# Linear attention with the values stationary in two column halves, denominators from running key sums, and new orders of all engines

## The chip, the cores and the metric

One NeuronCore of one Trainium2 chip runs the whole program. The metric is the device time of one execution in microseconds (us); lower is better. Matmuls run on PE (TensorE, weight loads shown as PEld), the other engines are DVE (VectorE), ACT (ScalarE), POOL (GpSimd) and SP (SyncE, which here only issues DMAs).

## The reference, cut to what matters

A small audio tower over 64 sequences of 256 frames (252 after a five-tap convolution), width 128: softmax attention with 8 heads and a top-2 mixture of 8 experts (layer 0), then a causal linear attention, a causal two-head attention and a dense mixture of 8 experts (layer 1). Only the linear attention is changed. In the notation of the reference:

```
q = elu(x @ W_q.T) + 1            # 8 heads of 16
k = elu(x @ W_k.T) + 1            # 8 heads of 16
v = x @ W_v.T                     # 8 heads of 64
num[t] = sum over s <= t of (q[t] . k[s]) * v[s]
den[t] = max(q[t] . (sum over s <= t of k[s]), 1e-6)
out = (num / den) @ W_out.T
```

## The kernel before, in words

Two sequences form a pair; a pair is 504 tokens in four tiles of 126 (TOK, TILES, TILE). There are 32 pairs. Everything before a pair's layers (the convolution and its normalisation) is done in a first phase; then three stretches follow: a start, 30 equal rounds, an end. A round works on four pairs at once: the softmax queries and keys of pair r+2 (letter q), the softmax attention of pair r+1 (a), the linear and the causal attention of pair r (l), and the experts' hidden chunks (h) and output chunks (o) of pairs r-1 and r+1.

Each engine has its own written-out order of these parts: a string of letters (SP_ROUND, POOL_ROUND, ACT_ROUND, DVE_ROUND, PE_ROUND and the same for START and END). Each letter runs the next step of that part's generator, up to its next `yield`; every engine works its steps strictly in that order, and counting semaphores join the engines. So a step that waits holds everything behind it on its engine. The letter w in PE_START is a filler matmul (L1713).

Steps that the prediction speaks of, by line:

- h on PE is three f16 matmuls of 504 columns into `pf` (L1315 to L1317, the helper `mm3`, which multiplies f32 numbers kept as a high and a low f16 half); ACT applies the GELU (L897), DVE casts the high half (L1285), POOL subtracts for the low half (L701).
- o on PE is four mm3 of 128 columns, 12 records, into bank 2 of `pf`. There is one such bank, so after an expert's last chunk the next expert's first chunk waits for DVE to add the bank to the residual (L1299, semaphore `gated`). An expert has four chunks in layer 1 and two in layer 0.
- Linear attention on PE, before: scores of four head blocks at a time (L1549, f16, 12 steps a pair, bank 0 of `pa1`). DVE multiplies the diagonal blocks by the causal mask (L1194), ACT copies the others (L845). Then eight steps of six f32 matmuls each (L1568) take the 126x126 factors as the stationary operand and 65 columns as the moving one: 64 value columns of one head and a column of ones, whose product is the denominator. DVE takes the denominator's maximum, its reciprocal and the product for every one of the eight (L1175, L1178, L1184) and writes `o1` with tokens on partitions.
- Output projection, before: four times, PE transposes 128 columns of `o1` (four f32 transposes, L1361), ACT writes the high half (L755), DVE the low half (L987), and PE multiplies by the output weights (L1315 to L1317 on `ot_hi`, `ot_lo`).
- POOL sets the column of ones each round (L685). The values come out of PSUM by ACT (L837).
- The causal attention's value product (L1645, `causal_values`) already has the form that the change brings to the linear one: for each key tile, the values of head 0 and of head 1, 64 columns each, are stationary in one half of the array's columns each, and write PSUM partitions 0 to 63 and 64 to 127.
- SP stores the high and low halves of queries and keys to DRAM and loads them spread over partitions (L494, L498, L504, L510). The softmax scores of the next round (L1422) wait for those of pair r+2. SP also issues the store of the output (L490).

## Time and profile before

| | us |
|---|---|
| median of 3 runs | 4110.01 (4109.32 to 4114.44) |
| the profiled execution, device time | 4117.0 |
| its span, first to last instruction | 4115.3 |
| mean granted PE clock | 0.994 |
| PE busy | 3969.7 (96%) |
| DVE busy | 3329.8 (81%) |
| ACT busy | 2840.7 (69%) |
| POOL busy | 2549.7 (62%) |

Busy time of PE counts a matmul from its start to its modelled end, and matmuls overlap in the pipeline. What a matmul costs is therefore the distance from its start to the next one's start, not its own duration.

### The profile page before, as it was taken

To read this page: it belongs to the slowest core of one execution; us is meant where nothing else is said; L and a number is where in the kernel's file an instruction comes from. 1 tells how busy PE (TensorE), PEld (TensorE's weight loads), DVE (VectorE), ACT (ScalarE), POOL (GpSimd) and SP (SyncE) were. 2 spreads that over 40 slices of the span, in tenths; PEclk is the share of its full clock that TensorE was granted. 3 is DMA by queue.
4 is the path that set the end of the run, shared out by engine and by line. 5 is a ranking of instruction groups with operands and counts; after the bars stand their busy time and mean duration, and the time that the engine had idled before them with its cause. 6 is when DMAs were issued, how large, how long until landed. Compare 5 with 4: busy or idle time off the path is not lost.

```text
span 4115.3 us, 104222 instructions
## 1 busy us (share of the span) xinstructions
PE 3969.7 (96%) x40901; PEld 2888.2 (70%) x40901; DVE 3329.8 (81%) x9263; ACT 2840.7 (69%) x4857; POOL 2549.7 (62%) x2496
## 2 busy tenths in 40 slices
PE   9889999999999999999999999999999999999988
PEld 4457677777767777777777777777777777777766
DVE  4478888888888888888888888888888888888866
ACT  4347777777777777777777677777767777777744
POOL 2246666666666666666666666666666666666646
PEclk9999999999999999999999999999999999999989
DMA  6111110001111010111101011110001111001100
GB/s 183 46 29 29 32 32 27 22 17 32 32 32 32 20 28 17 32 32 32 32 17 30 18 32 32 32 32 17 22 27 32 32 32 31 17 19 29 30 16 6
DMA packets 137273, 127.63 MB, mean 31 GB/s; under 512 B 29008, under 2 KB 135568, under 8 KB 136784
## 3 DMA queue, kind: packets, MB, share of 16 engines
q1 hardware_dynamic: 136784, 120.97, 10.2%
q8 instruction: 324, 5.31, 0.5%
q14 instruction: 165, 1.35, 0.1%
HBM read 71.12 MB, written 49.55 MB: 29 GB/s over the span
## 4 chain that ended last, share of the span: by engine, by line
PE 70%; DVE 20%; DMA 3%; SPq 2%; issue 2%; ACT 2%; POOL 1%; DVEq 0%; ACTq 0%
PE pf L1315 12%; PE pf L1317 11%; PE pf L1316 11%; PE pa L1568 9%; DVE h L1299 4%; PE pa L1460 3%; PE pa L1361 3%; DVE hid_hi L1285 3%; PE pa L1315 3%; PE pa L1317 3%; PE pa L1316 3%; PE pa L1549 3%; PE pa L1446 3%; DVE row_max L1247 2%; SPq L510 2%
## 5 line engine op out<-in xcount | busy, mean ns | idle before, releaser
L701 POOL TENSOR_TENSOR hid_lo<-hid,hid_hi 128x504 f16<-128x504 f32 x1536 | 1789.2, 1179 | 889.5 <-DVE hid_hi L1285 888.6
L897 ACT ACTIVATE hid<-pf,vec 128x504 f32<-128x504 f32 x1536 | 1025.2, 678 | 505.8 <-PE pf L1317 454.1
L1315 PE MATMUL pf<-w_hi,hid_hi 128*126 128x128 f16 x6144 | 1147.2, 225 | 42.4 <-DVE h L1299 38.3
L1317 PE MATMUL pf<-w_hi,hid_lo 128*126 128x128 f16 x6144 | 1121.9, 221 | 0.0
L1316 PE MATMUL pf<-w_lo,hid_hi 128*126 128x128 f16 x6144 | 1121.5, 221 | 0.0
L1315 PEld LDWEIGHTS pf<-w_hi,hid_hi 128*126 128x126 f16 x6144 | 843.5, 137 | 197.8 <-DVE h L1299 106.1
L1285 DVE CAST hid_hi<-hid 128x504 f16<-128x504 f32 x1536 | 799.1, 540 | 87.4 <-ACT hid L897 87.0
L1316 PEld LDWEIGHTS pf<-w_lo,hid_hi 128*126 128x126 f16 x6144 | 845.4, 138 | 30.3
L1317 PEld LDWEIGHTS pf<-w_hi,hid_lo 128*126 128x126 f16 x6144 | 847.4, 138 | 0.0
L1299 DVE SCALAR_TENSOR_TENSOR h<-pf,gates,h 126x128 f32<-126x128 f32 x2048 | 572.8, 342 | 52.7 <-PE pf L1317 52.5
L665 POOL TENSOR_TENSOR pt<-pt,band 126x262 f32<-126x262 f32 x512 | 358.6, 716 | 373.0 <-ACT pt L803 372.9
L1315 PE MATMUL pf<-xf_hi,w_hi 128*128 128x504 f16 x1536 | 579.2, 377 | 2.3 <-DVE xf_lo L1269 1.1
L1317 PE MATMUL pf<-xf_hi,w_lo 128*128 128x504 f16 x1536 | 577.9, 376 | 0.0
L1316 PE MATMUL pf<-xf_lo,w_hi 128*128 128x504 f16 x1536 | 577.8, 376 | 0.0
L1568 PE MATMUL pa<-v,pt 126*126 126x65 f32 x3072 | 391.4, 278 | 1.5 <-DVE o L1184 1.4
L1568 PEld LDWEIGHTS pa<-v,pt 126*126 126x126 f32 x3072 | 365.0, 193 | 18.4 <-issue 18.3
L803 ACT ACTIVATE pt<-pa 126x504 f32<-126x504 f32 x512 | 278.4, 589 | 139.0 <-PE pa L1446 138.0
L1092 DVE TENSOR_REDUCE minus_max<-pa 126x2 f16<-126x504 f32 x512 | 329.6, 682 | 19.1 <-PE pa L1422 15.9
L897 ACT ACT_TABLE_LOAD x247 | 316.9, 1283 | 4.4
L1317 PEld LDWEIGHTS pf<-xf_hi,w_lo 128*128 128x128 f16 x1536 | 150.0, 98 | 177.5 <-issue 1.3
L1175 DVE TENSOR_SCALAR den<-pa 126x4 f32<-126x4 f32 x256 | 40.9, 160 | 252.9 <-PE pa L1568 251.2
L1194 DVE TENSOR_TENSOR pt<-pa,causal 126x504 f32<-126x504 f32 x256 | 173.3, 677 | 64.2 <-PE pa L1549 62.7
(215 smaller groups left out, 7431.0 us busy)
## 6 DMA issues: line engine op xcount, KB each, us to landing
qk_spread<-terms SPq DMA_DIRECT2D x224, 126.0 KB, 2.6
qk_spread<-terms SPq DMA_DIRECT2D x192, 63.0 KB, 2.3
y_scratch<-hid SPq DMA_DIRECT2D x32, 252.0 KB, 2.1
y_in<-y_scratch SPq DMA_DIRECT2D x32, 252.0 KB, 3.2
terms<-qk_hi SPq DMA_DIRECT2D x32, 252.0 KB, 2.3
terms<-qk_lo SPq DMA_DIRECT2D x32, 252.0 KB, 2.4
qk_spread<-terms SPq DMA_DIRECT2D x32, 252.0 KB
terms<-ot_hi SPq DMA_DIRECT2D x32, 252.0 KB, 2.4
```

The costliest lines, as they stand in the source:

```text
L665: nc.gpsimd.tensor_tensor(strip, strip, band[0:TILE], ALU.mult).then_inc(S0["p_band"], 1)
L701: nc.gpsimd.tensor_tensor(hid_lo[:, c % 8], hid[:, c % HIDS], hid_hi[:, c % 8], ALU.subtract).then_inc(hid_lo_done[c % 2], 1)
L803: nc.scalar.activation(pt[0][0:TILE, i % 8], pa0[0:TILE, i % 2, 0:TOK], ACT.Exp, scale=HEAD ** -0.5).then_inc(S0["p_exp"], 1)
L897: nc.scalar.activation(hid[:, c % HIDS], pf[:, c % 2, 0:TOK], func, bias=vec[:, bias:bias + 1]).then_inc(F["hid_ready"], 1)
L1092: nc.vector.tensor_reduce(minus_max[0:TILE, 2 * b:2 * b + 2, hd // 2, 64 * (hd % 2) + MAX_ROW], pa0[0:TILE, i % 3, 0:TOK].rearrange("p (t ...
L1194: nc.vector.tensor_tensor(pt[1][0:TILE, i % 4].rearrange("p (t q) -> p t q", t=4), pa1[0:TILE, 0, 0:TOK].rearrange("p (t q) -> p t q", t=4 ...
L1285: nc.vector.tensor_copy(hid_hi[:, c % 8], hid[:, c % HIDS]).then_inc(F["hid_hi_done"], 1)
L1299: last = nc.vector.scalar_tensor_tensor(h[0:TILE, i], pf[0:TILE, 2, i * D:(i + 1) * D], gates[0:TILE, kind, i, e:e + 1], h[0:TILE, i], ALU ...
L1315: nc.tensor.matmul(out, ah, bh, start=start, stop=False, skip_group_check=skip)
L1316: nc.tensor.matmul(out, ah, bl, start=False, stop=False, skip_group_check=skip)
L1317: return nc.tensor.matmul(out, al, bh, start=False, stop=stop, skip_group_check=skip)
L1568: last = nc.tensor.matmul(pa1[0:TILE, 1, first:first + wide], factors[:, cols(blk)], v1[0:TILE, 2 * b + kt, hd], start=(t == 0), stop=(t = ...
```

## The change

The scores, the masks and the products with the weights stay. What is new:

- The value product is turned: the values (64 columns of one head, f32) are stationary, two heads in the two column halves, and the factors (126 columns) move. The output has value columns on partitions and tokens along the bank, so it needs no transposes before the output projection. Four steps a pair instead of eight, each of 12 f32 matmuls.
- The denominators come ahead of the attention: PE transposes the keys, ACT and DVE split them in f16 halves, PE multiplies them by a 0/1 matrix `later` (running sums), DVE multiplies by the queries, PE sums over each head's 16 rows by a 0/1 matrix `head_of`, DVE takes maximum and reciprocal once, POOL widens each to 64 columns, PE transposes them (16 f32 transposes) and ACT copies them to `spread_inv`. DVE then divides a whole bank at once, ACT writes the high halves and POOL the low halves.
- The value projections stand between these steps, in banks (1, 1, 1, 0).
- The gate's step semaphores are merged into one (same instructions, same order). New constants are built on POOL at the start.
- All order strings are rewritten (the letters of a round are the same in number but for l: PE 54 to 53, ACT 35 to 40, DVE 47 to 42, POOL 6 to 13).

```diff
-SP_ROUND = ("llallqqoqq")
+SP_ROUND = ("llalloqqqq")
-POOL_ROUND = ("llhhhhlhhhahhhhaaaaaahaaahhhahaaaaaahhhhhahlhhhhhhhlhlhhhqhhhhhhhhhhhhhhh")
+POOL_ROUND = ("llhhhhhhhhllllhhahhaaaaaaaaaalaahhllhaalahahhlhhhhahhlhhlhhhhhhhhhhqhhhhhhhhhhhh")
-ACT_ROUND = ("hhhlhlhllhhlhlhhhlhhllhhalaaaaaaalaahaaalhhaaaahallahhllhhahhhlalhhhllhllahhhahhqhlhqhhqhlllllql"
-             "hlqlhlhhllhhlhh")
+ACT_ROUND = ("hhhlhlhllhhhlhllhllhllhlllhhaalaaaalaalaalaalhhalaalaahhhhahlalhhhlhllalahhahhhahhlhhhhllllqhlhh"
+             "lhqlhhlqlhhlqqlhhhlh")
-DVE_ROUND = ("lalhahaaohlhaahllllallhaahoaaahaahaahhaaaalolhlhhlllhlllhllllhahllolhlalahqlahalaholllhhhhoalhhh"
-             "ahoalahoalhhoqqhhhlollqohlllholhhoqhhlhqlolhqlhohhlho")
+DVE_ROUND = ("llhhahaaoalhaahllllllalhhlohlaahaaaaahaahaalaalhhllolhllllllhalohhhlllhhqahoalahaahhhoahalaaholh"
+             "hahlohhllohhlhollholqqhhhohhqlhhohlqolqlohhqhohl")
-PE_ROUND = ("hhaoohoaohhlaohllhaolohhlaohlhaolaoaohhaaaolahlhalllooallaaalllhallhaallloollhhallaaaloaloahlalh"
-            "lahllloohlhohohooahlohaohllhlloohhoohoohahaoohqlhlohohloqhohloqohlqlollolhlohloqlhoholhhloo")
+PE_ROUND = ("hhohaoohaohlaohllhaooohlhlhllalhllaolalhalloalahlaahloolalalhhlaalalalaaloollloolhaalaallhllhhao"
+            "haoooalhoahhlhllloooahhahohoohohahaooohllohloohhloohoqohloohlhhllohlhqloqhlqoolhoohqlhohol")
```

On POOL:

```diff
-                counted = n(p)
-                pool.wait_ge(started, 1)
-                pool.wait_ge(S1["h_biased"], counted)
-                nc.gpsimd.memset(v1[0:TILE, :, :, LIN_VALUE:LIN_VALUE + 1], 1.0).then_inc(S1["v1_ones"], 1)
-                yield
+                for i in range(TILES):
+                    if i == 0:
+                        pool.wait_ge(S1["inv_ready"], n(p + 1))
+                    nc.gpsimd.tensor_copy(wide[i].rearrange("p (h d) -> p h d", h=HEADS),
+                                          inv_den[0:TILE, i].unsqueeze(2).to_broadcast([TILE, HEADS, LIN_VALUE])
+                                          ).then_inc(S1["inv_wide"], 1)
+                    yield
+                for quad in range(4):
+                    b, g = quad // 2, quad % 2
+                    pool.wait_ge(S1["o1_hi"], n(p * 4 + quad + 1))
+                    part = (slice(None), slice(2 * g, 2 * g + 2), slice(b * SEQ, (b + 1) * SEQ))
+                    nc.gpsimd.tensor_tensor(ot_lo[1][part], fs1[:, quad % 2, 0:TOK].rearrange("p (c q) -> p c q", c=2),
+                                            ot_hi[1][part], ALU.subtract).then_inc(S1["o1_lo"], 1)
+                    yield
```

On ACT (`values_high` runs four times, as `high` did):

```diff
+            def values_high(p, quad):
...
+                act.wait_ge(S1["o1_norm"], n(p * 4 + quad + 1))
+                nc.scalar.copy(ot_hi[1][:, 2 * g:2 * g + 2, b * SEQ:(b + 1) * SEQ],
+                               fs1[:, quad % 2, 0:TOK].rearrange("p (c q) -> p c q", c=2)
+                               ).then_inc(S1["o1_hi"], 1)
...
+                act.wait_ge(S1["keys_turned"], n(p + 1))
+                nc.scalar.copy(keys_hi, pa1[0:TILE, 0, 0:TILES * D]).then_inc(S1["keys_high"], 1)
+                yield
...
+                for k in range(4):
+                    act.wait_ge(S1["spread_raw"], n(p * 4 + k + 1))
+                    nc.scalar.copy(spread_inv[:, k], pa1[:, 1 - k % 2, 0:TOK]).then_inc(S1["spread_ready"], 1)
                     yield
...
-                for c in range(4):
-                    high(1, p * 7 + 1 + c, ot_hi[1][:, c % 2])
-                    yield
```

On DVE (the old `divide` ran eight times, the new one runs four times):

```diff
+                dve.wait_ge(S1["keys_high"], n(p + 1))
+                nc.vector.tensor_tensor(keys_lo, pa1[0:TILE, 0, 0:TILES * D], keys_hi,
+                                        ALU.subtract).then_inc(S1["keys_low"], 1)
+                yield
+                dve.wait_ge(S1["sums_raw"], n(p + 1))
+                nc.vector.tensor_tensor(q_sums, pa1[:, 0, 0:TOK], fs1[:, 0, 0:TOK], ALU.mult
+                                        ).then_inc(S1["sums_ready"], 1)
+                yield
+                dve.wait_ge(S1["den_raw"], n(p + 1))
+                nc.vector.tensor_scalar(den[0:TILE], pa1[0:TILE, 0, 0:TILES * HEADS], 1e-6, None, ALU.max
+                                        ).then_inc(S1["den_done"], 1)
+                dve.wait_ge(S1["den_done"], n(p + 1))
+                nc.vector.reciprocal(inv_den[0:TILE].rearrange("p t h -> p (t h)"), den[0:TILE]
+                                     ).then_inc(S1["inv_ready"], 1)
+                yield
+
+                def divide(quad):
+
+
+                    dve.wait_ge(S1["av_done"], n(p * 4 + quad + 1))
+                    dve.wait_ge(S1["o1_lo"], n(p * 4 + quad - 1))
+                    nc.vector.tensor_tensor(fs1[:, quad % 2, 0:TOK], pa1[:, 1, 0:TOK], spread_inv[:, quad], ALU.mult
                                             ).then_inc(S1["o1_norm"], 1)
...
-                for c in range(4):
-                    low(1, p * 7 + 1 + c, ot_lo[1][:, c % 2], ot_hi[1][:, c % 2])
-                    yield
```

On PE (the four steps of the value projection stand before, between and after these; that of the sums runs for both sequences):

```diff
+                pe.wait_ge(S1["el_map"], n(p * 2 + 2))
+                for i in range(TILES):
+                    last = nc.tensor.transpose(pa1[0:TILE, 0, i * D:(i + 1) * D], fs1[:, 1, cols(i)], ident[:])
+                last.then_inc(S1["keys_turned"], 1)
...
+                pe.wait_ge(S1["keys_low"], n(p + 1))
+                for b in range(2):
+                    for kt, first, width in ((0, 0, SEQ), (1, TILE, TILE)):
+                        for keys in (keys_hi, keys_lo):
+                            last = nc.tensor.matmul(pa1[:, 0, b * SEQ + first:(b + 1) * SEQ],
+                                                    keys[:, (2 * b + kt) * D:(2 * b + kt + 1) * D],
+                                                    later[0:TILE, 0:width], start=(kt == 0 and keys is keys_hi),
+                                                    stop=(kt == 1 and keys is keys_lo), skip_group_check=True)
...
+                pe.wait_ge(S1["sums_ready"], n(p + 1))
+                for i in range(TILES):
+                    last = nc.tensor.matmul(pa1[0:TILE, 0, i * HEADS:(i + 1) * HEADS], q_sums[:, cols(i)], head_of[:],
+                                            start=True, stop=True)
...
+                for k in range(4):
...
+                    for c in range(2):
+                        for t in range(2):
+                            first = c * SEQ + t * TILE
+                            last = nc.tensor.transpose(pa1[:, 1 - k % 2, first:first + TILE],
+                                                       wide[2 * b + t][:, (2 * g + c) * D:(2 * g + c + 1) * D],
+                                                       ident[0:TILE, 0:TILE])
...
+                        pe.wait_ge(S1["at_ready"], n(p * 8 + 2 * quad + 2))
+                        pe.wait_ge(S1["o1_norm"], n(p * 4 + quad))
+                        off = pt[1][0:TILE, 3 * quad % 4]
+                        for c in range(2):
+                            diagonal = pt[1][0:TILE, (3 * quad + 1 + c) % 4]
+                            for t, (kt, qt) in enumerate(((0, 0), (0, 1), (1, 1))):
+                                for odd in range(2):
+                                    factors, blk = (off, 2 * c + odd) if t == 1 else (diagonal, 2 * odd + kt)
+                                    first = c * SEQ + qt * TILE
+                                    last = nc.tensor.matmul(pa1[64 * odd:64 * odd + 64, 1, first:first + TILE],
+                                                            v1[0:TILE, 2 * b + kt, 4 * g + 2 * c + odd],
+                                                            factors[:, cols(blk)], start=(t < 2), stop=(t != 1),
+                                                            skip_group_check=True)
...
-                        turn(1, p * 7 + 1 + c, o1_rows[:, :, c * 128:(c + 1) * 128])
...
+                for c in range(4):
+                    pe.wait_ge(S1["o1_lo"], n(p * 4 + 3 + c // 2))
```

## Rows read from the trace of the kernel before

**Rows 1.** The page: busy us (share of the span) xinstructions of each engine.
```profile
PE 3969.7 (96%) x40901; PEld 2888.2 (70%) x40901; DVE 3329.8 (81%) x9263; ACT 2840.7 (69%) x4857; POOL 2549.7 (62%) x2496
```
**Rows 2.** Timeline, transposes that open a pair's work, one round apart (start, duration).
```profile
1994.52 0.60 PE L1392 MATMUL pa<-ident,pt 128*126 128x128 f32 x4
...
2114.97 0.60 PE L1392 MATMUL pa<-ident,pt 128*126 128x128 f32 x4
```
**Rows 3.** Timeline of PE: the old value product between two score steps.
```profile
2052.75 1.48 PE L1568 MATMUL pa<-v,pt 126*126 126x65 f32 x12
2054.07 0.39 PE L1549 MATMUL pa<-qk_spread 128*126 128x126 f16 x4
```
**Rows 4.** Timeline of PE: four f32 transposes and what follows them.
```profile
2081.86 0.59 PE L1361 MATMUL pa<-ident,o 126*128 126x126 f32 x4
2082.29 0.64 PE L1361 MATMUL pa<-ident,xn 126*128 126x126 f32 x4
```
**Rows 5.** Timeline of PE: the causal value product, in two column halves.
```profile
2010.35 0.86 PE L1645 MATMUL pa<-fs,v 126*64 126x252 f32 x8
2011.14 0.27 PE L1315 MATMUL pf<-w_hi,hid_hi 128*126 128x128 f16 x1
```
**Rows 6.** Timeline of PE: 504-column f16 records, then a half-height form.
```profile
2002.78 0.38 PE L1316 MATMUL pf<-xf_lo,w_hi 128*128 128x504 f16 x1
2002.99 0.38 PE L1317 MATMUL pf<-xf_hi,w_lo 128*128 128x504 f16 x1
2003.30 0.49 PE L1618 MATMUL pa<-pt 64*126 64x126 f32 x4
```
**Rows 7.** Groups by line and form (count | busy us, mean ns | idle before).
```profile
L1175 DVE TENSOR_SCALAR den<-pa 126x4 f32<-126x4 f32 x256 | 40.9, 160 | 252.9 <-PE pa L1568 251.2
L1178 DVE RECIPROCAL inv_den<-den 126x4 f32<-126x4 f32 x256 | 45.6, 178 | 8.8
L1184 DVE TENSOR_TENSOR o<-pa,inv_den 126x256 f32<-126x256 f32 x256 | 108.6, 424 | 8.8
L1299 DVE SCALAR_TENSOR_TENSOR h<-pf,gates,h 126x128 f32<-126x128 f32 x2048 | 572.8, 342 | 52.7 <-PE pf L1317 52.5
L987 DVE TENSOR_TENSOR ot_lo<-pa,ot_hi 128x504 f16<-128x504 f32 x192 | 128.2, 681 | 55.4 <-ACT ot_hi L755 50.6
L755 ACT ACTIVATE ot_hi<-pa 128x504 f16<-128x504 f32 x192 | 109.8, 588 | 132.1 <-PE pa L1361 119.4 <-PE pa L1645 12.5
L897 ACT ACT_TABLE_LOAD x247 | 316.9, 1283 | 4.4
L677 POOL COPY h<-h 126x512 f32<-126x512 f32 x32 | 19.5, 608 | 3.0 <-DVE h L1299 3.0
L701 POOL TENSOR_TENSOR hid_lo<-hid,hid_hi 128x504 f16<-128x504 f32 x1536 | 1789.2, 1179 | 889.5 <-DVE hid_hi L1285 888.6
```
**Rows 8.** Who waited for whom: us in total, times, longest.
```profile
PEld pf L1315 <- DVE h L1299: 106.1, 228, 1.8
PEld pa L1376 <- DVE gate_terms L1027: 45.9, 61, 1.7
```
**Rows 9.** Timeline: softmax keys of one pair, from projection to the scores.
```profile
2007.77 0.38 PE L1315 MATMUL pa<-w_hi 128*128 128x504 f16 x1
...
2015.72 0.73 DVE L1075 SCALAR_TENSOR_TENSOR qk_lo<-pa,vec,qk_hi 128x504 f16<-128x504 f32 x1
...
2016.48 0.36 SPq L498 DMA_DIRECT2D terms<-qk_lo  x1
...
2017.46 1.12 SPq L490 DMA_DIRECT2D out<-h  x2
2018.63 3.22 SPq L504 DMA_DIRECT2D qk_spread<-terms  x5
...
2025.66 0.43 PE L1422 MATMUL pa<-qk_spread 64*126 64x252 f16 x4
```
**Rows 10.** A stretch near the end: us, busy (x) of PE, PEld, DVE, ACT, POOL, clock, DMA, GB/s.
```profile
3980.00:3990.00 10.00, 9.17 (x58) 8.41 (x59) 4.14 (x11) 1.17 (x3) 1.14 (x1) 0.59 0.00 0
```

More of the change, by code:

```diff
@@ L878, in linear_and_causal_attention @@
                     yield
-                high(1, p * 7 + 6, ot_hi[1][:, 0])
+                high(1, p * 3 + 2, ot_hi[1][:, 0])
                 yield
@@ L1148, in linear_and_causal_attention @@
                 yield
-                low(1, p * 7, xt_lo[1][:], xt_hi[1][:])
+                low(1, p * 3, xt_lo[1][:], xt_hi[1][:])
                 yield
@@ L1265, in linear_and_causal_attention @@
                     yield
-                low(1, p * 7 + 6, ot_lo[1][:, 0], ot_hi[1][:, 0])
+                low(1, p * 3 + 2, ot_lo[1][:, 0], ot_hi[1][:, 0])
                 yield
@@ L1554, in linear_and_causal_attention @@
                         yield
-                    if (i - 1) % 3 and i > 1:
-                        quad, part = (i - 1) // 3, (i - 1) % 3
-                        g8 = 2 * quad + part - 1
-                        b, wide = quad // 2, LIN_VALUE + 1
-                        pe.wait_ge(S1["at_ready"], n(p * 8 + g8 + 1))
-                        pe.wait_ge(S1["o1_norm"], n(p * 8 + g8))
-                        off, diagonal = pt[1][0:TILE, 3 * quad % 4], pt[1][0:TILE, (i - 1) % 4]
-                        for m in range(2):
-                            hd = 4 * (part - 1) + 2 * m + quad % 2
-                            for qt, terms in ((0, ((0, diagonal, 2 * m),)),
-                                              (1, ((0, off, hd // 2), (1, diagonal, 2 * m + 1)))):
-                                first = (2 * m + qt) * wide
-                                for t, (kt, factors, blk) in enumerate(terms):
-                                    last = nc.tensor.matmul(pa1[0:TILE, 1, first:first + wide], factors[:, cols(blk)],
-                                                            v1[0:TILE, 2 * b + kt, hd], start=(t == 0),
-                                                            stop=(t == len(terms) - 1))
```

250 lines of the change are left out of this document (135 added, 115 removed).

## The prediction

> **What bounds the kernel now.** First the page: PE is busy for 96% of the span, the next engine, DVE, for 81% [rows 1]. That is not yet proof, because busy spans of PE overlap. So second, the timeline of PE, read for distances from start to start. The 504-column records follow each other every 0.21 us, the old value product every 0.110 us (12 records from 2052.75 to 2054.07), f32 transposes every 0.108 us (four in 0.43 us) [rows 3, 4, 6]. Third, one round lasts 120.45 us (1994.52 to 2114.97) [rows 2]. Pricing every step of PE's order for a round by such distances (48 h at 0.64, 48 o at 0.69, and so on) I get 114 us of streaming. So about 6 us of a round, 5%, are waits and the rest is throughput: what PE no longer streams should come off the time almost whole, as long as the waits don't grow. Fourth, the waits. PE's largest are for the eviction of an expert's bank by DVE, 106 us in 228 stops, and for the gate's terms, 46 us in 61 stops [rows 8].
>
> **The change part by part, per pair of sequences, on PE.**
> Removed: eight value steps of 12 records, 96 x 0.110 = 10.56 us [rows 3]; four times four transposes of the result, 16 x 0.108 = 1.73 us [rows 4]. Together 12.29.
> Added, the value product in halves: 96 records again, since an f32 matmul shows as two. The causal attention already does this. Its eight records (four of 252 columns, four of 126) take 0.79 us to the next start [rows 5]. At the f32 transposes' rate of 0.108 us per 126 columns, one after the other they would take 12 x 0.108 = 1.30 us; in pairs 0.65. So two heads do run beside each other, and the missing 0.14 us is the entry and exit. So 48 pairs at 0.108 = 5.18 us, and 0.05 us for each of four entries whose loads nothing covers, 0.20. The bound from above is no pairing, 10.4 us.
> A change of the array's layout costs by itself: the step from a 504-column record to a half-height form takes 0.31 instead of 0.21 us [rows 6]. Writing both PE_ROUND strings out as steps I count 43 such changes in a round before and 47 after: 4 x 0.10 = 0.40 us. The Trainium skill (TensorEngine Tiling, Key Properties) says that changing the tiling mode drains TensorE. A full drain would be about one record's length, 0.27 us, and the sum would get 0.7 us a round worse; the rows show 0.10 and I go by them.
> Added, the denominators: four f32 transposes of the keys, 4 x 0.108 = 0.43. The running sums are four f16 matmuls of 252 and four of 126 columns at half and a quarter of 0.21 us [rows 6], 0.63. The sum over heads is four f32 matmuls, eight records with only 8 columns, but a full f32 weight load each; the old value product with 65 columns was held to 0.110 us by the same load, so 0.88. The spread of the reciprocals is 16 transposes, 1.73. Together 3.67.
> PE: 12.29 - 5.18 - 0.20 - 0.40 - 3.67 = 2.84 us less a pair.
>
> **The other engines, per pair** [rows 7]. DVE: away go 8 x (160 + 178 + 424) and 4 low halves at 681, 8.82 us; new are four whole-bank divisions, the keys' low half and the product with the queries, six at about 681, and two small ones, 4.43 us. DVE loses 4.4 us and falls to about 79%. ACT: four high halves (588) go; the keys' high half, four copies of reciprocals and four high halves come, nine at 588, +2.94. But its order groups the functions better. Counting the switches between the exponential and the two GELUs in the two ACT_ROUND strings gives 15 table loads a round before and 13 after, 2 x 1.28 = -2.57. ACT stays level. POOL: four copies at about 608 and four subtractions at 1179 come, +7.0 us after the memset is taken off, so 62% goes to about 69%. None of these becomes the bound; they cost nothing on the sum while PE has other work to do, and the orders put h, o and a between. If that cover were gone the new chain ahead of the attention (transpose, ACT, DVE, PE, DVE, PE, DVE, POOL, PE, ACT) would stand open with about 8 us. It replaces the old chain of four times transpose, ACT, DVE. The output projection now waits for a subtraction on POOL, behind whatever hidden chunk POOL is in, up to 1.18 us each; by my count of steps the third of its four parts has 3.2 us of cover for 2.7 us of division, copy and subtraction. The first parts need only three of the four subtractions.
> The new semaphores and constants add nothing that PE waits for; the constants are built in the first phase.
>
> **What is late next.** Three places by the step counts of the new PE order:
> (a) Between an expert's last chunk and the next expert's first, the old order always has at least 1.24 us of other work; the new one has 0.64 and 0.97 us at two places. That is +0.9 us a round, for DVE's four additions alone take 4 x 0.342 = 1.4 us [rows 7], or a little less where they overlap.
> (b) The softmax gate: from its logits to its turn there were 10.6 us of other work, now 5.3, for a chain of some fifteen small DVE and ACT steps; at 0.16 to 0.42 each, with a table load of 1.28 [rows 7], an estimate of about 6 us: +0.7. The other gate's cover grows from 2.6 to 3.3: -0.5.
> (c) DVE, 4.4 us lighter, evicts sooner. The waits for it are 106 us over 32 pairs, 3.3 a pair [rows 8]; I take a fifth of them off, -0.6. The bounds are 0 and -3.3.
> Waits together: +0.5 us.
>
> **Sum.** 2.84 - 0.5 = 2.34 us a round; 30 rounds, 70 us. The start and the end hold one linear attention each, but there PE also waits for its chain: in the end stretch the granted clock averages 0.59, so it stood at the lower of its two levels (1.2 of 2.4 GHz) most of the time, over 10 us while PE shows 58 records and DVE, ACT and POOL little [rows 10]; I take 3 us for each, 6. In all -76 us against the profiled execution's 4117.0 us, 4041; the median is 7 us lower, so 4034.
>
> **Rivals.**
> 1. *The softmax keys arrive late* (slower). After the keys' projection the old order has 16.4 us of PE work by my prices before the next round's first scores, and 17.9 in the trace (2007.77 to 2025.66) [rows 9]. The new order has 11.7. The path there is: low half on DVE 7.95 us after the projection began, 0.73 for it, 5.4 until SP has issued all loads, of which 1.12 are the output's stores, now moved ahead of it, and the landing, in the 3.8 us left. If ACT and DVE reach the keys as late as before and landing takes 2.6 of these 3.8, the path is 15.6 us and PE waits 3.9 us at the scores, in every round. That beats the 2.34 gained by 1.6 us, so 4110 + 47, about 4157. It decides from a wait of 2.3 us. Against it: in the new strings ACT takes queries and keys one after the other, and DVE has only two steps between their low halves; at the earliest the path is 2.3 + 4.3 + 2.6 = 9.2 us, which the 11.7 cover. Chance 0.1.
> 2. *The new waits take the gain and no more* (same). The linear chain now runs over POOL twice and ACT nine times. Two more places open by 1.2 us each bring it to within 0.2%, about what a measurement can tell from no change: 4102 to 4118. Chance 0.06.
> 3. *The halves don't pair* with 126 columns and f32 loads: 48 x 0.108 = 5.2 us more a round than forecast, 2.9 slower than before, 4196. The rows speak clearly against it [rows 5]: 0.02.
> 4. *The waits shrink too*, because DVE's relief reaches all of its evictions and the gate's turn finds its terms ready: 2.84 + 2 a round, 150 us, about 3965. Chance 0.15.
> The forecast holds the rest, 0.67, itself between about 3995 and 4075, that is a change of waits from -0.8 to +1.9 us a round.
>
> **How the numbers follow.** The predicted time is the forecast's, 4034. The range 3970 to 4100 takes the forecast's own, most of rival 4 and the near side of rival 2; outside stay rivals 1 and 3 and the far end of 4. Faster by over 0.2%: the forecast and rival 4, and a little of rival 1, 0.83. Same: 0.06. Slower: 0.11.
>
> **What would show it.** A round of about 118.1 us between those opening transposes. The new value product at about 1.5 us for 24 records, starts in pairs a few ns apart and 0.108 us from pair to pair. DVE near 3190 us busy, POOL near 2775, ACT near 2850 with some 60 table loads fewer. PE's waits for the bank's eviction still its largest. I am wrong in the mechanism if the value records follow singly at 0.108, and wrong in the balance if the first softmax scores wait for a DMA, the gate's turn waits by over 2 us, or the spread or the output projection waits for POOL.

## The result, and the profile after

The changed kernel takes 3989.8 us (median of 4, 3986.9 to 3990.8) where the kernel before took 4109.7 beside it: ratio 0.9708, 95% interval 0.9694 to 0.9723, about 120 us faster. The forecast was 4034 with a range of 3970 to 4100. The sign and the range hold; the gain is 44 us larger than forecast.

The profile of the changed kernel, busy time by engine, answers to [rows 1]:

```profile
span 3989.1 us, 105187 instructions
PE 3827.6 (96%) x41541; PEld 2742.8 (69%) x41541; DVE 3155.2 (79%) x8623; ACT 2855.2 (72%) x4958; POOL 2782.1 (70%) x2725
PEclk9999999999999999999999999999999999999999
```

The reader is to see that PE keeps its 96%: it still sets the pace. DVE at 3155 (I said 3190), POOL at 2782 (2775) and ACT at 2855 (2850) came as worked out. The transposes that open a pair's work, one round apart, answer to [rows 2] (start, duration):

```profile
2068.90 0.60 PE L1435 MATMUL pa<-ident,pt 128*126 128x128 f32 x4
...
2186.13 0.60 PE L1435 MATMUL pa<-ident,pt 128*126 128x128 f32 x4
```

That round is 117.23 us. Over 28 rounds (from the fourth opening to the thirty-second) the mean is 120.60 us before and 117.24 after: 3.36 us a round, where I had 2.34. 28 rounds make 94 us of the 126 us by which the two profiled spans differ (4115.3 and 3989.1). The stretch from the last of these openings to the end went from 311.4 to 278.6 us, another 33; the start didn't change (427.0 and 427.7 us).

The new value product between two score steps, timeline of PE, answers to [rows 3]:

```profile
2123.89 0.43 PE L1489 MATMUL pa<-qk_spread 64*126 64x252 f16 x4
2124.25 1.51 PE L1653 MATMUL pa<-pt,v 126*64 126x126 f32 x24
2125.69 0.43 PE L1489 MATMUL pa<-qk_spread 64*126 64x252 f16 x4
```

24 records take 1.44 us to the next start; before, 12 took 1.32 [rows 3]. A pair of records costs 0.108 us, the halves run beside each other.

Who waited for whom (us in total, times, longest), answers to [rows 8]:

```profile
PEld pf L1358 <- DVE h L1342: 161.2, 262, 2.3
PEld pa L1419 <- DVE gate_terms L1067: 1.6, 4, 0.7
PEld pa L1465 <- DMA qk_spread<-terms: 12.6, 14, 3.5
PEld pa L1503 <- POOL pt L679: 7.6, 34, 1.0
```

The wait for an expert's bank grew (106 before). The wait for the gate's terms is gone (45.9 before). The first softmax scores wait for a DMA 14 times in the whole run, so rival 1's wait exists but doesn't come in every round. The spread waits for POOL for 0.9 us in the whole run, the output projection not at all.

**Where a round's time went.** I charge each record of PE with the time until the next one starts, and sum by line over the 28 rounds. A wait so falls to the record ahead of it. Us a round:

| step | before | after | change | predicted |
|---|---|---|---|---|
| linear value product (L1568, L1653) | 10.80 | 5.77 | -5.03 | -5.18 |
| turns of the result (L1361) | 1.79 | 0 | -1.79 | -1.73 |
| keys' turns, running sums, head sums, spread | 0 | 0.44 + 0.65 + 0.90 + 1.94 | +3.93 | +3.67 |
| four more layout changes (estimate, see below) | | 4 x 0.092 | +0.37 | +0.40 |
| all else | | | -0.84 | +0.5 |
| round | 120.60 | 117.24 | -3.36 | -2.34 |

The steps that the change touches come to -2.52, 0.3 less than forecast. "All else" went the other way than I had it, by 1.3 us, and that is 38 us of the run.

"All else" mixes streaming and waits. To part them I price each step of PE, and each move from one step to the next, with the spacing that the fastest twentieth of its kind (same shapes, same neighbour) shows over both kernels and the runs below (all but the two with fillers). What is left of the round are waits. Us a round:

| kernel | round | streaming | waits |
|---|---|---|---|
| before | 120.6 | 113.5 | 7.1 |
| after | 117.2 | 110.6 | 6.6 |
| e7_turn_alone | 118.9 | 109.6 | 9.3 |
| e12_gates_later | 123.1 | 113.5 | 9.6 |
| e2_thin_denominators | 116.9 | 108.0 | 8.9 |
| e9_thin_both | 116.2 | 108.0 | 8.3 |

The split is an estimate: with the fastest quarter in place of the twentieth the waits are 0.2 us lower in every row, and their differences stay. So the change took 2.9 us of streaming a round (2.84 forecast) and the waits fell by 0.5 where I had them grow by 0.5.

### The profile page after: what moved, and what is told of

Read it like the earlier page. It is cut to its first block, busy times and chain, and to the rows that moved or that the text cites. A ratio compares the mean times of both kernels' runs of the same rounds, so it can differ in the third digit from the quotient of the medians.

```text
span 3989.1 us, 105187 instructions
## 1 busy us (share of the span) xinstructions
PE 3827.6 (96%) x41541; PEld 2742.8 (69%) x41541; DVE 3155.2 (79%) x8623; ACT 2855.2 (72%) x4958; POOL 2782.1 (70%) x2725
## 4 chain that ended last, share of the span: by engine, by line
PE 71%; DVE 16%; ACT 6%; POOL 3%; issue 2%; DMA 1%; SPq 1%; ACTq 0%; DVEq 0%
PE pf L1358 12%; PE pf L1360 11%; PE pf L1359 11%; PE pa L1653 5%; DVE h L1342 4%; PE pa L1358 4%; PE pa L1359 4%; PE pa L1360 4%; PE pa L1503 3%; PE pa L1635 3%; DVE hid_hi L1328 3%; PE pa L1489 2%; ACT hid L935 2%; PE pa L1404 2%; PE pa L1465 2%
## 5 line engine op out<-in xcount | busy, mean ns | idle before, releaser
L935 ACT ACTIVATE hid<-pf,vec 128x504 f32<-128x504 f32 x1536 | 1021.1, 680 | 447.9 <-PE pf L1360 407.2
L1358 PE MATMUL pf<-w_hi,hid_hi 128*126 128x128 f16 x6144 | 1127.4, 224 | 88.0 <-DVE h L1342 79.0
L1360 PE MATMUL pf<-w_hi,hid_lo 128*126 128x128 f16 x6144 | 1108.7, 221 | 0.0
L1359 PE MATMUL pf<-w_lo,hid_hi 128*126 128x128 f16 x6144 | 1108.5, 221 | 0.0
L1328 DVE CAST hid_hi<-hid 128x504 f16<-128x504 f32 x1536 | 765.6, 521 | 95.7 <-ACT hid L935 89.4
L1231 DVE TENSOR_TENSOR fs<-pa,o 128x504 f32<-128x504 f32 x128 | 87.3, 682 | 237.6 <-PE pa L1653 237.4
L647 POOL TENSOR_TENSOR rstd<-ve,minus_half 126x4 f32<-126x4 f32 x128 | 142.0, 1109 | 119.0 <-DVE ve L1020 119.0
L1358 PEld LDWEIGHTS pf<-xf_hi,w_hi 128*128 128x128 f16 x1536 | 155.2, 101 | 75.7 <-ACT hid L935 34.9
```

What stands on the lines that cost most here:

```text
L935: nc.scalar.activation(hid[:, c % HIDS], pf[:, c % 2, 0:TOK], func, bias=vec[:, bias:bias + 1]).then_inc(F["hid_ready"], 1)
L1328: nc.vector.tensor_copy(hid_hi[:, c % 8], hid[:, c % HIDS]).then_inc(F["hid_hi_done"], 1)
L1358: nc.tensor.matmul(out, ah, bh, start=start, stop=False, skip_group_check=skip)
L1359: nc.tensor.matmul(out, ah, bl, start=False, stop=False, skip_group_check=skip)
L1360: return nc.tensor.matmul(out, al, bh, start=False, stop=stop, skip_group_check=skip)
```

## The experiments

Twelve kernels ran, each timed against the kernel before. "Round" is the mean of the 28 rounds, "tail" the stretch from the last of them to the end.

| run | built on | us | ratio, 95% interval | round | tail |
|---|---|---|---|---|---|
| before | | 4109.7 | 1 | 120.60 | 311.4 |
| after | | 3989.8 | 0.9708 (0.9694 to 0.9723) | 117.24 | 278.6 |
| e1_unpaired | after | 4024.4 | 0.9778 (0.9763 to 0.9792) | 118.36 | 280.7 |
| e2_thin_denominators | after | 3981.2 | 0.9688 (0.9673 to 0.9702) | 116.90 | 279.1 |
| e8_thin_max | after | 3989.4 | 0.9689 (0.9675 to 0.9704) | 117.26 | 278.8 |
| e9_thin_both | after | 3956.2 | 0.9608 (0.9592 to 0.9624) | 116.22 | 277.9 |
| e4_evict_first | after | 3991.6 | 0.9696 (0.9681 to 0.9710) | 117.26 | 279.0 |
| e5_thin_pool | after | 4004.9 | 0.9749 (0.9733 to 0.9765) | 117.77 | 280.8 |
| e7_turn_alone | before | 4050.1 | 0.9840 (0.9825 to 0.9855) | 118.91 | 296.6 |
| e10_before_thin_max | before | 4109.2 | 0.9984 (0.9975 to 0.9994) | 120.63 | 306.8 |
| e11_turn_thin_max | before | 4044.9 | 0.9825 (0.9811 to 0.9840) | 118.75 | 295.5 |
| e12_gates_later | before | 4187.9 | 1.0181 (1.0166 to 1.0196) | 123.11 | 310.8 |
| e3_end_fillers | before | 4113.6 | 0.9992 (0.9983 to 1.0002) | 120.72 | 305.2 |
| e13_turn_and_fillers | before | 4052.7 | 0.9855 (0.9839 to 0.9872) | 118.82 | 300.2 |

The kernel before took between 4108.6 and 4115.3 us (medians) beside these, so compare ratios or rounds, not the times.

**Do the halves pair because they alternate?**

```diff
-for t, (kt, qt) in enumerate(((0, 0), (0, 1), (1, 1))):
-    for odd in range(2):
+for odd in range(2):
+    for t, (kt, qt) in enumerate(((0, 0), (0, 1), (1, 1))):
```

> The changed kernel, with the value product's two column halves no longer alternating: within each block column all six records of the one half come first, then the six of the other. Theory (the halves run beside each other only when they alternate): the step of 24 records goes from about 1.44 us to 2.3 to 2.6 us, 3.5 to 4.6 us more a pair, so 3990 + 105 to 140 = 4095 to 4130 us. Rival (a half-width f32 record costs half of a full one by itself, whoever stands beside it): no change, 3985 to 3995 us. The granted clock in the end stretch is read beside it: the changed kernel keeps 1.00 there.

Timeline of PE, the same 24 records now issued in runs to one half:

```profile
2141.86 1.78 PE L1653 MATMUL pa<-pt,v 126*64 126x126 f32 x24
```

The time, 4024, lies between both forecasts. The product takes 1.71 us a step instead of 1.44 (6.83 a round instead of 5.77), far from the 2.6 of no pairing. The starts within one step (ns after the first: 0, 159, 267, 272, 374, 431, 482, 538, and so on to 1294, 1401, 1507) still interleave; only the first two records and the last two stand alone. So the pairing needs no strict alternation. The rival falls too: where a record of one half stands alone, the next start is 0.107 us away, as for a full-width one, so half the width doesn't make a record cheaper by itself. This run can't price a whole product without pairing. What it does show is that 1.06 us more streaming in this part of the round (55 to 73 us behind the opening) made the round 1.12 us longer: there added streaming passes to the time in full. It doesn't show that streaming taken off there would.

**The turned value product alone.** The kernel before with its value product turned and in halves; its result comes out in another layout than what follows reads, and the denominators are clamped at 1e6, so the linear attention's output isn't computed.

```diff
-last = nc.tensor.matmul(pa1[0:TILE, 1, first:first + wide], factors[:, cols(blk)],
-                        v1[0:TILE, 2 * b + kt, hd], ...)
+last = nc.tensor.matmul(pa1[64 * m:64 * m + 64, 1, qt * TILE:(qt + 1) * TILE],
+                        v1[0:TILE, 2 * b + kt, hd, 0:LIN_VALUE], factors[:, cols(blk)], ...)
```

> The kernel before with its own orders, denominators from nothing, transposes and all other engines' work, but each value step turned: values stationary in two column halves, factors moving, 12 records in 6 pairs (what DVE reads from the bank is then not numerator and denominator; the clamp is 1e6 to keep numbers finite). It tells how much the turned product gives alone. Theory: 12 x 0.110 = 1.32 us a step becomes 6 x 0.108 + 0.05 + two changes of layout 0.2 = 0.90, 3.4 us less a pair, 30 rounds 100 us; and if the clock in the end stretch stays up as in the changed kernel, 20 to 25 us more: 3985 to 4010 us. Rival A (the end stretch has nothing to do with the value product's form): 4005 to 4015 us, clock at 0.6 to 0.8 there as before. Rival B (the gain is in the new orders, not in the product): 4080 to 4110 us.

None of the three forecasts holds; 4050 lies between them. The product itself falls by 3.8 us a round (10.80 to 6.99), the round by 1.69. The rest came back as waits (7.1 to 9.3 in the table above). The waits of the weight loads in this run:

```profile
PEld pf L1315 <- DVE h L1299: 98.0, 239, 1.8
PEld pa L1376 <- DVE gate_terms L1027: 52.0, 61, 1.8
PEld pa L1460 <- POOL pt L665: 47.6, 95, 1.0
PEld pa L1549 <- DVE pt L1194: 44.4, 131, 1.3
```

The last two are the softmax attention's value product, waiting for its factors, and the linear attention's scores; in the kernel before their waits were 10.1 and 8.7 us. That they come late because the product ahead of them is short fits, but wasn't tried. So in the old orders more than half of the product's gain is lost. The rest of the change adds work on PE (its own steps come to -2.52, not -3.8) and yet takes the round down by another 1.67 us. This gap of 3 us a round lies in the new orders and in DVE's lighter load. The next runs ask which.

**Is it DVE's relief?** The maximum over the keys reads half of them (the maximum only shifts the exponents). That takes 0.26 us from each of 16 maxima, 4.1 us a pair; the change itself took 5.5 us a pair from DVE (3329.8 to 3155.2 in all).

```diff
-pa0[0:TILE, i % 3, 0:TOK].rearrange("p (t k) -> p t k", t=2),
+pa0[0:TILE, i % 3, 0:TOK].rearrange("p (t k) -> p t k", t=2)[:, :, 0:TILE],
```

> The changed kernel with VectorE's maximum over the keys taken over the first 126 of 252 keys (the subtracted maximum only shifts the exponents, so what is computed stays the same up to rounding). Theory A, VectorE and TensorE bind together in the first part of a round: the change took TensorE work and VectorE work out together, and each alone brings little. Then half of the maxima's time, some 0.26 us x 16 = 4 us a pair, brings 0.5 to 1.5 us a round now (3945 to 3975 us), since TensorE's own 110.9 us of streaming and the other waits are left. Rival B, TensorE's order alone binds and VectorE's busy share is a symptom: under 0.3 us a round, 3980 to 3992.

> The kernel before with the maximum over half of the keys, nothing else. Theory A: it shows what VectorE's relief alone is worth with the old value product; some 0.5 to 2 us a round, 4050 to 4095. Rival B: under 0.3 us a round, 4100 to 4110.

> The kernel before with the turned value product alone (as in the earlier run of that, 4050 us, whose streaming fell by 4.4 us a round while its waits rose by 2.7) and with the maximum over half of the keys. Theory A: the waits that rose there are for VectorE, so the relief takes most of the 2.7 us off: 3960 to 3990. Rival B: they are the order's own (an operand a step later, ScalarE's or GpSimd's), and the relief brings what it brings to the kernel before: 4030 to 4050.

The 4.4 and 2.7 us that it names for e7 are 3.8 and 2.1 by the table above.

Groups by line, count, busy us and mean ns, the maxima in the changed kernel and then in e8_thin_max:

```profile
L1133 DVE TENSOR_REDUCE minus_max<-pa 126x2 f16<-126x504 f32 x512 | 326.1, 676 | 11.7 <-PE pa L1465 10.2
```

```profile
L1133 DVE TENSOR_REDUCE minus_max<-pa 126x2 f16<-126x252 f32 x512 | 198.5, 417 | 72.7 <-PE pa L1465 72.7
```

The reader is to see both ends of the line: DVE works 128 us less on the maxima and sits 61 us longer waiting for PE's scores. The round is 0.02 us longer after, 0.03 longer before and 0.16 shorter with the turned product. Theory A falls in all three: DVE's busy share of over 90% in the first part of the round (44.5 of the 49 us in the first row of the windows below) is not a bound by itself. The 6 us that e10 gains lie in start and tail. One thing is left open: these runs relieve DVE at the softmax maxima. The change relieves it elsewhere, in the steps between the linear attention's products, and a relief there alone was not tried.

**Does thinner work on PE help there?** The denominators' part on PE is cut (two turns of the keys instead of four, one image and one tile of the running sums, one tile of head sums, a quarter of each spread; ACT's copy of the reciprocals scales them by 1e-6), so the linear attention's denominators aren't computed.

```diff
-for i in range(TILES):
+for i in (0, 3):
...
-for b in range(2):
-    for kt, first, width in ((0, 0, SEQ), (1, TILE, TILE)):
+for b in range(1):
+    for kt, first, width in ((0, 0, TILE),):
...
-for c in range(2):
-    for t in range(2):
+for c in range(1):
+    for t in range(1):
```

> The changed kernel with PE's part of the denominators thinned, all waits and all work of other engines kept: 2 of 4 key transposes, 2 f16 matmuls of 126 columns of 8, 1 of 4 f32 sums over heads, 4 of 16 transposes of the reciprocals (so the denominators are not the reference's; scale and clamp keep the numbers finite). Taken off PE: 0.22 + 0.54 + 0.66 + 1.30 = 2.7 us a pair. Theory (PE's streaming sets the round, so it comes off whole): 3990 - 75 to 87 = 3903 to 3915 us. Rival (the chain of the linear attention sets the round): 3970 to 3990 us.

These steps fell from 3.93 to 1.65 us a round, the round by 0.34, inside the rival's range. What came in their place, waits of the weight loads; first the changed kernel, then e2, then the two cuts together (e9):

```profile
PEld pa L1465 <- DVE minus_max L1133: 49.5, 133, 0.8
```

```profile
PEld pa L1465 <- DVE minus_max L1133: 79.2, 133, 1.1
```

```profile
PEld pa L1465 <- DVE minus_max L1133: 47.7, 101, 0.8
```

> The changed kernel with the maximum over half of the keys and with the thinned denominators (TensorE's four layout changes cut to one, the running sums to one image and one tile, the head sums to one tile; the denominators are then not those of the reference). Theory A: the thinned denominators brought 0.34 us a round alone because VectorE is behind just there; with VectorE relieved, their 2.5 us of streaming comes off nearly in full, so that both together bring more than the sum of the two alone, 2.5 to 4 us a round: 3870 to 3915. Rival B: the sum of the two alone and no more, about 3970 to 3980.

Together they take 1.02 us off the round, where the two alone sum to 0.32. So the form of theory A holds (they bind together) and its size doesn't: I expected 2.5 to 4. With both cut, PE's waits are still 8.3 us a round against 6.6 in the changed kernel (table above): other steps are late next. Windows of the changed kernel, the first 49 us of the round and the rest (us, busy of PE, PEld, DVE, ACT, POOL, clock, DMA, GB/s):

```profile
2068.90:2117.90 49.00, 47.99 (x471) 33.15 (x470) 44.53 (x132) 36.59 (x63) 31.63 (x32) 1.00 0.21 59
2117.90:2186.10 68.20, 65.58 (x808) 49.89 (x807) 51.74 (x137) 51.38 (x91) 54.44 (x53) 1.00 0.02 6
```

The denominators' steps stand in the first stretch, 38 to 50 us behind the opening: there 2.28 us less on PE give 0.34 us, 0.15 of it. In the second stretch, what e1 adds counts in full. Adding work in the first and taking it off in the second were not tried on the new orders; on the old ones e7 took 3.8 us off the value product and got 1.69.

**The largest wait.** In the round shown PE waits 2.0 us near 2183 for an expert's bank, whose eviction on DVE stands behind a cast. Letters 109 and 110 and letters 113 and 114 of DVE's round change places, so that the eviction comes first.

```diff
-"hahlohhllohhlhollholqqhhhohhqlhhohlqolqlohhqhohl"
+"hahlohhllohhlohllohlqqhhhohhqlhhohlqolqlohhqhohl"
```

> The changed kernel with two letters of DVE_ROUND exchanged at two places (positions 109 and 110, 113 and 114, counted from 0): DVE adds an expert's bank before it casts the next hidden chunk. PE stands still for 2.0 and 0.75 us a round for these two additions. Theory (the wait at an expert's boundary is DVE's order, and a late cast delays nobody at once): 1.3 to 2 us less a round, 3990 - 40 to 60 = 3930 to 3950 us. Rival (the cast's chain, ACT, DVE, POOL, PE, is as urgent, so the wait moves on to the output chunk that needs it): 3980 to 4000 us.

Nothing: 117.26, and the time is the rival's. PE's own stops in the run, first in the changed kernel and then in this one:

```profile
PE pf L1358 <- DVE h L1342: 79.0, 66, 2.1
PE pf L1358 <- POOL hid_lo L724: 8.7, 29, 0.5
```

```profile
PE pf L1358 <- DVE h L1342: 41.3, 66, 2.1
PE pf L1358 <- POOL hid_lo L724: 39.0, 60, 0.7
```

The stops for the eviction fall by 38 us and those for the low halves, which follow the cast, grow by 30: the cast is as late as the eviction was early, and PE needs both.

**Is it POOL?** The eight new steps of POOL are cut to a few columns, so the spread reciprocals and the result's low halves aren't computed in full (ACT's copy of the reciprocals scales them by 1e-6 here too).

```diff
-wide[i].rearrange("p (h d) -> p h d", h=HEADS)
+wide[i].rearrange("p (h d) -> p h d", h=HEADS)[:, :, 0:1]
...
+few = (slice(None), slice(0, 2), slice(0, 4))
+nc.gpsimd.tensor_tensor(ot_lo[1][part][few], ...)
```

> The changed kernel with POOL's eight new steps cut to a few columns each, waits kept (reciprocals and low halves are then wrong): 6 to 7 us less of POOL a pair. Theory (POOL's 70% have cover everywhere): 3980 to 3990 us. Rival (POOL's additions lengthen DVE's casts, which in the trace take 0.41 us alone and up to 1.4 us beside a POOL operation, and delay low halves that PE waits for): 3930 to 3970 us, and the mean cast falls from 521 ns.

POOL's load is no bound: with less of it the round is 0.53 us longer, outside both forecasts, and the mean cast is 520 ns against 521. PE's transposes of the normalised rows wait longer for ACT's output (the loads' wait at that line goes from 23.1 us to this):

```profile
PEld pa L1406 <- ACT xn L788: 39.1, 64, 2.5
```

The traces show why. Laid record by record over the changed kernel's, PE's round is the same up to 84.4 us behind the opening. There these transposes come 0.44 us late, and everything behind them 0.5. Six us ahead of that place, on DVE and POOL, the changed kernel and then this one:

```profile
2146.93 0.69 DVE L1328 CAST hid_hi<-hid 128x504 f16<-128x504 f32 x1
2147.54 0.68 DVE L1250 TENSOR_TENSOR h<-pa,h 126x512 f32<-126x512 f32 x1
2146.47 0.86 POOL L679 TENSOR_TENSOR pt<-pt,band 126x262 f32<-126x262 f32 x1
```

```profile
2149.19 1.35 DVE L1330 CAST hid_hi<-hid 128x504 f16<-128x504 f32 x1
2150.46 0.68 DVE L1252 TENSOR_TENSOR h<-pa,h 126x512 f32<-126x512 f32 x1
2149.12 1.14 POOL L726 TENSOR_TENSOR hid_lo<-hid,hid_hi 128x504 f16<-128x504 f32 x1 [0.48 <-DVE hid_hi L1330]
```

The cast stands beside whatever POOL does: in the changed kernel the rest of a short operation; here, with POOL's own steps gone and its order run ahead, a whole subtraction. It takes about 1.35 us instead of 0.69 in every one of the 28 rounds. DVE's addition behind it comes 0.7 us later, and with it the normalisation (POOL, ACT) that PE's transposes wait for. So the rival had the right mechanism, the casts, and the wrong sign: less work on POOL moved it to a worse place beside them.

**Are the gates' waits worth what they show?** In the kernel before, one letter of each gate's turn and of the product behind it goes one step later.

```diff
-"lahllloohlhohohooahlohaohllhlloohhoohoohahaoohqlhlohohloqhohloqohlqlollolhlohloqlhoholhhloo"
+"lahllloohlhohohooahlohaohllhlloohhoohoohhaoaohqlhlohohloqhohloqohlqlollolhlohloqlhohohlholo"
```

> The kernel before with both gates' turns one hidden chunk (three 504-column records, 0.64 us) later in TensorE's round, and the product behind them one step later; nothing else is moved. In the kernel before the two turns wait for the gates' terms, 0.9 us a round together; in the changed kernel these waits are gone. Theory A: this is part of the gain that I had not in my sum (I had +0.2 us a round there): the waits fall by 0.6 to 0.9 us a round and the time to 4085 to 4095. Rival B: the wait moves on to the next late step, as with the exchanged evictions, and the time stays within 5 us of before.

Neither: 2.5 us a round slower (PE's waits go from 7.1 to 9.6). Waits of DVE and of the loads in this run:

```profile
DVE h L1053 <- PE pa L1384: 56.6, 60, 2.0
PEld pf L1315 <- DVE h L1299: 171.4, 283, 2.2
PEld pa L1376 <- DVE gate_terms L1027: 22.9, 31, 1.1
```

The gates' wait does halve (45.9 to 22.9). But DVE, in its own written order, now stands at the addition of the gates' product (L1053) until PE has it, and the evictions queued behind that addition come late: PE's wait for the banks goes from 106.1 [rows 8] to 171.4 us. 0.6 us of delay at each of two gates in one engine's order costs 2.5 us a round when the other orders stay. The new kernel has no such wait at the gates, and all its orders were written anew together. That is as near as these runs come to placing the 3 us: a relief of DVE was tried by itself and gave nothing, but the new orders can't be separated from the new steps, so that the orders hold the 3 us is argued and not shown.

**The end.** Windows of the kernel before and of the changed one where the last linear attention runs (same columns):

```profile
3990.00:4000.00 10.00, 10.00 (x70) 9.67 (x69) 4.39 (x14) 1.52 (x3) 2.28 (x2) 0.56 0.01 2
4000.00:4010.00 10.00, 7.60 (x64) 7.20 (x63) 4.45 (x13) 0.90 (x2) 0.71 (x1) 0.79 0.00 0
```

```profile
3880.00:3890.00 10.00, 9.10 (x123) 6.99 (x119) 6.33 (x11) 4.53 (x9) 5.10 (x5) 1.00 0.01 2
3890.00:3900.00 10.00, 9.55 (x137) 8.00 (x135) 7.85 (x19) 2.69 (x5) 8.05 (x7) 1.00 0.02 5
```

The granted clock, below 0.8 in four such rows before (with [rows 10], and 0.70 at 4010 to 4020), stays at 1.00. On the chain that ended last a value step took this long, before and after (start, us):

```profile
3985.75 2.45 PE pa L1568 x12
3994.67 2.56 PE pa L1568 x12
```

```profile
3883.89 1.46 PE pa L1653 x24
```

The eight steps on that chain add up to 17.9 us (1.3 to 2.8 each), the four new ones to 5.9. From the first scores to the turn for the causal attention it is 49.8 us before (3978.98 to 4028.76) and 28.2 after (3875.47 to 3903.66). To tell the clock from the work, filler matmuls that no one reads keep PE running in the stretch (40 of 504 columns, 8.5 us by [rows 6]).

```diff
+def unused_at_end():
+    ...
+        nc.tensor.matmul(pa0[:, 0, 0:TOK], W("up1", 0, 128)[0], W("up1", 0, TOK)[0], start=True, stop=True)
```

> The kernel before with 40 filler matmuls of 504 columns in PE's end order, two behind each score and value step of the last pair's linear attention. They compute nothing that is used. Theory (the end stretch is long because PE's clock falls to its lower level there): the clock stays near 1.00, the stretch loses about 20 to 25 us and pays up to 8 us of fillers where PE has no wait to put them in: 4090 to 4098 us. Rival (the clock is only a sign, the stretch is bound by the chain over DVE and ACT): 4110 to 4118 us.

> The kernel before with the turned value product alone and with the 40 filler matmuls of 504 columns in the end stretch. The stretch from the last round to the end took 311.4 us before, 305.2 with the fillers alone, 296.6 with the turned product alone, 278.6 changed. Theory A, the end's gain is the product's halved streaming with the granted clock's share on top, and the rest is the shorter chain of turns: with fillers the clock is at 1.00 and the stretch takes 292 to 298 us, since the fillers' own 8.5 us eats what the clock gives back. Rival B, the lower clock is what costs in the end: under 288 us.

With the fillers the clock is 1.00 there in both runs. The rows of e3:

```profile
3990.00:4000.00 10.00, 10.00 (x104) 8.56 (x102) 5.98 (x17) 1.84 (x3) 2.29 (x2) 1.00 0.01 2
4000.00:4010.00 10.00, 8.97 (x81) 7.11 (x80) 4.21 (x14) 0.58 (x1) 1.14 (x1) 1.00 0.01 2
```

The tail falls by 6.2 us with the fillers, by 14.8 with the turned product, and with both it is 300.2: 3.6 more than the product alone, as the fillers cost more than the clock then gives back. The whole run of e3 stayed within 0.1% of before, in its rival's range; e13 missed both forecasts, theory A's upper end by 2 us. Counting all the fillers as exposed, and as delaying nothing else, the lower clock costs (an estimate) at most 6.2 + 8.5 = 15 us before, and at most 8.5 - 3.6 = 5 us with the turned product. So of the 33 us in the tail, 15 are the shorter product with what the clock does on it. The other 18 came with the rest of the change: about 2 are the share of regular work behind the last opening, and the turns of the result with ACT and DVE in series behind them (4013.1 to 4022.3 on the old chain, some 9 us) are the piece of the old chain that is gone. That last share was not tried by itself.

## Why the prediction was right, and where its sizes failed

- **PE's own steps** (-2.84 a round): right, -2.52 by the spacings charged to them and -2.9 in the split of streaming and waits. The value product (5.77 against 5.38), the denominators (3.93 against 3.67) and the turns are each within 10%. The two traces have the 43 and 47 layout changes a round that I counted. From a 504-column record into a half-height form the next start is 0.304 us away, where another 504-column record would be at 0.211; from the 126-column scores into such a form it is 0.150 instead of 0.057. That is 0.093 us in both, near the 0.10 of my sum. The Trainium skill (TensorEngine Tiling (Array Packing), Key Properties) says that a mode change drains TensorE; read as a full record, that would have been 0.27, and the trace shows a third of it.
- **Step (b), the gates** (+0.7 - 0.5): the step that failed. I summed a chain of small operations, about 6 us, against 5.3 us of cover and took a new wait. The row says 45.9 us of waits before and 1.6 after. Over the 28 rounds the two spacings ahead of the gates' turns sum to 1.52 us a round before and to 0.27 after, which is what they take when nothing waits: -1.25 where I had +0.2. I counted cover in PE's order alone and left out where DVE's order puts the chain; e12 shows that the cost of a late gate mostly lies in DVE's order.
- **Step (a), the experts' boundaries** (+0.9) and **step (c), DVE's relief** (-0.6): their sum was +0.3. The stops of PE for the bank's eviction grew from 38.3 to 79.0 us in all, +1.3 a pair, so the cover did shrink as counted and no relief showed. e8, e10 and e11 agree: 4 us less on DVE a pair are worth 0 to 0.16. Gates and banks thus come to about 0 together. The waits' other 0.6 us lie in smaller stops: all but gone are PE's 15.7 us for DVE at the causal attention's transposes (L1634) and 10.6 us for a DMA at the linear scores (L1549), new are 8.7 us for POOL's low halves. That the first two would go was not in my sum; as far as the forecast is concerned it is luck.
- **The end** (-3 us): a large miss, about -29 measured apart from the rounds' share. I had the row with the clock at 0.59 before me [rows 10] and priced the stretch as a regular round's gain. Most of its old value steps took 2.35 to 2.8 us at the lower clock, and there were eight in series, so the product alone is 17.9 - 5.9 = 12.0 us less. The **start** (-3) gave nothing.
- Together, with the opening at four fifths of a round (so that the start holds 0.8 and the tail 1.2 of the thirty rounds): 30.6 us in the rounds and 25.7 at the end too little, 6.3 at the start too much, 50 in all: 4041 forecast for the profiled execution, 3990.8 measured. Against the medians it is 44, since the profiled execution before lay 7 us over its median and the one after 1.
- **Table loads**: I counted some 60 fewer. ACT has 464 in the kernel before and 405 in the changed one, 59 fewer: right, as ACT's busy time is. 29 of them are gone at the GELU of the hidden chunks (247 to 218 at L897 and L935), 30 at the softmax exponentials (90 to 60).
- **Rivals.** 1 (softmax keys): 14 stops in the run, not every round. 2: new waits do exist, but the old ones went. 3: excluded by the step's 1.44 us. 4 (waits shrink too, 3965): the measured 3990 lies between it and the forecast, nearer to it, and 5 us outside the forecast's own 3995. One of its two reasons holds, the gate's turn finds its terms ready; the other, DVE's relief, doesn't.

## What to carry to other kernels

Price a removed step where it stands. Streaming of TensorE taken off gave 0.15 of itself in one part of the round (e2) and 0.44 in another with the old orders (e7), while streaming added (e1) cost all of itself: a run that lengthens a step is no price for shortening it. Where every engine has an order written by hand, a step shortened or moved in one order alone loses its gain to the others (-3.8 gave -1.7; two steps 0.6 later gave +2.5), so rewrite all orders in the same change. Price the thin ends of a kernel by their own rows, with their granted clock, not by the regular round's.

## What the runs showed of the hardware that was not expected

**VectorE's casts stand still beside GpSimd.** The cast of a hidden chunk (L1328, SBUF to SBUF, f32 to f16) has a median of 0.414 us but a mean of 0.521, and takes up to 1.38. Timelines of DVE and POOL in the changed kernel, at the 2.0 us stop:

```profile
2182.94 1.36 DVE L1328 CAST hid_hi<-hid 128x504 f16<-128x504 f32 x1
```

```profile
2181.67 2.35 POOL L724 TENSOR_TENSOR hid_lo<-hid,hid_hi 128x504 f16<-128x504 f32 x2 [1.54 <-DVE hid_hi L1328]
```

The cast ends at 2184.30, 0.28 us after POOL's subtraction (2184.02). Of the 1536 casts, 264 take over 0.6 us. Each of them starts while an operation of POOL runs (765 do) and ends 0.276 to 0.284 us after that operation; of the 771 that start with POOL idle none is that long. Not every operation of POOL does this. Its powers over 4 or 16 elements a partition (L647, L717) last 1.1 us and more, and 187 casts start and end inside one of them without stretching. The evictions of the same engine, which read PSUM, don't stretch either, though 1632 of the 2048 start beside an operation of POOL (duration ns, min/median/max):

```profile
L1342 DVE SCALAR_TENSOR_TENSOR h<-pf,gates,h x2048: 332/341/353, 205.9 to 3985.8; 126x128 f32<-126x128 f32 x187
```

The Trainium skill (SBUF — State Buffer, "SBUF: two separate sides") calls the port pair that the two engines share an exclusive lock for the whole instruction, for VectorE where an operation runs in a 2-port mode or has two SBUF inputs. No run here shows in which mode the cast runs. The casts beside POOL's wide operations agree with it; the 187 beside its powers don't. The stretching is 0.107 us x 1536, about 165 us or 5% of DVE's busy time, that isn't work. That the lock is the cause was not tested by a run. What one such stretch can be worth e5 shows: a cast 0.66 us longer, at a place with a chain behind it, made the round 0.53 us longer.

**Column halves overlap without alternation**, partners six records apart in the program (e1): a step of 24 records takes 1.71 us instead of 1.44, not 2.6.
